# Output projection of a tile pair in seven block products instead of eight, with sums of rows and their low parts on VectorE

## The reference, cut to what matters

```
q, k, v = heads(x @ Wq + bq), heads(x @ Wk + bk), heads(x @ Wv + bv)     # 16 heads of 32
scores = where(mask == 0, -inf, einsum(q, k) / sqrt(32))
out = einsum(softmax(scores), v)                                        # back to 128 x 64 x 512
return layernorm(x + out @ Wo + bo)                                     # no gain, no shift, eps 1e-5
```

## Time and profile before

| | |
|---|---|
| median of 3 runs | 822.24 us (821.85 to 822.4) |
| profiled execution: its own time | 821.39 us |
| its span | 819.5 us |
| granted TensorE clock, mean | 0.999 |
| TensorE matmul busy | 812.0 us, 99% |
| VectorE, GpSimd, ScalarE busy | 544.9, 512.6, 238.2 us |

### The profile page before, as it was taken

How to read it: one execution, slowest core, us unless ns; L and a number is a source line. 1 busy time by engine, 2 the same in 40 slices (tenths; PEclk the granted TensorE clock), 3 DMA queues, 4 the chain that set the end, 5 groups by cost and what they waited for, 6 DMA issues and landing times.

```text
span 819.5 us, 25422 instructions
## 1 busy us (share of the span) xinstructions
PE 812.0 (99%) x11286; PEld 665.1 (81%) x11286; DVE 544.9 (66%) x691; ACT 238.2 (29%) x315; POOL 512.6 (63%) x407
## 2 busy tenths in 40 slices
PE   9999999999999999999999999999999999999997
PEld 7788888888888888888888888888888888888886
DVE  5667667766567666676665776656766567766795
ACT  6532233221332222332223322133322233223223
POOL 1386667656675565856658566576665767657682
PEclk9999999999999999999999999999999999999999
DMA  9224424253342433424334243352424434234342
GB/s 321 90 79 122 120 81 135 84 143 95 88 143 72 149 92 92 139 70 142 105 91 134 71 144 95 82 154 82 128 88 106 136 82 131 84 108 118 105 105 104
DMA packets 50173, 92.37 MB, mean 113 GB/s; under 512 B 11280, under 2 KB 13328, under 8 KB 47888
## 3 DMA queue, kind: packets, MB, share of 16 engines
q1 hardware_dynamic: 47568, 87.08, 36.2%
q10 hardware_dynamic: 2496, 3.67, 1.6%
HBM read 40.37 MB, written 16.78 MB: 70 GB/s over the span
## 4 chain that ended last, share of the span: by engine, by line
PE 98%; DVE 1%; POOL 0%; ACT 0%; issue 0%; POOLq 0%; DVEq 0%
PE ring L289 23%; PE ring L291 21%; PE ring L290 21%; PE ring L386 7%; PE ring L387 7%; PE ring L390 7%; PE psum_s L357 6%; PE ring L375 6%; PE ring L407 1%; PE ring L309 0%; POOL soft L912 0%; PE ring L313 0%; PE ring L317 0%; DVE soft L717 0%; DVE top L724 0%; ACT soft L568 0%
## 5 line engine op out<-in xcount | busy, mean ns | idle before, releaser
L912 POOL TENSOR_TENSOR soft<-soft,top 128x1024 f32<-128x1024 f32 x62 | 125.2, 2020 | 77.5 <-DVE top L724 77.5
L171 POOL TENSOR_TENSOR soft<-soft,inverse 128x1024 f32<-128x1024 f32 x62 | 118.9, 1918 | 24.9 <-DVE inverse L731 22.2
L563 ACT ACTIVATE kt<-ring,bk 128x512 f32<-128x512 f32 x64 | 43.6, 681 | 258.7 <-PE ring L291 258.6
L889 POOL TENSOR_TENSOR x_lo<-x_raw,x_hi 128x512 fp32r<-128x512 f32 x56 | 72.0, 1286 | 61.1 <-ACT x_hi L548 61.1
L289 PE MATMUL ring<-wv_hi,x_hi 128*128 128x512 f32 x256 | 103.5, 404 | 0.0
L289 PE MATMUL ring<-x_hi,wk_hi 128*128 128x512 f32 x256 | 103.1, 403 | 0.0
L728 DVE TENSOR_REDUCE total<-soft 128x16 f32<-128x1024 f32 x62 | 75.6, 1219 | 41.0 <-ACT soft L568 41.0
L291 PE MATMUL ring<-wv_hi,x_lo 128*128 128x512 f32 x256 | 100.1, 391 | 0.0
L291 PE MATMUL ring<-x_hi,wk_lo 128*128 128x512 f32 x256 | 99.9, 390 | 0.0
L290 PE MATMUL ring<-x_lo,wk_hi 128*128 128x512 f32 x256 | 99.7, 390 | 0.0
L290 PE MATMUL ring<-wv_lo,x_hi 128*128 128x512 f32 x256 | 99.6, 389 | 0.0
(11 more groups left out here) (81 smaller groups left out, 1362.3 us busy)
## 6 DMA issues: line engine op xcount, KB each, us to landing
pt<-soft SPq DMA_DIRECT2D x464, 64.0 KB, 2.0
x_raw<-in_xt SPq DMA_DIRECT2D x15, 1024.0 KB, 6.8
row<-in_x SPq DMA_DIRECT2D x60, 256.0 KB, 2.7
out_rows<-row SPq DMA_DIRECT2D x60, 256.0 KB, 2.6
adj<-in_adj SPq DMA_DIRECT2D x16, 128.0 KB, 2.9
pt<-soft ACTq DMA_DIRECT2D x32, 64.0 KB, 2.2
kt<-in_wk SPq DMA_DIRECT2D x4, 256.0 KB, 5.1
row<-in_wv SPq DMA_DIRECT2D x1, 1024.0 KB, 8.4
```

What stands on the lines that cost most here:

```text
L171: ops.tensor_tensor(soft_of(c), soft_of(c), on_keys(inverse[:, c % 2, :]), ALU.mult).then_inc(normed, 1)
L889: nc.gpsimd.tensor_tensor(x_lo[:, buf, :, rows], x_raw[:, :, rows], x_hi[:, buf, :, rows].bitcast(F32), ALU.subtract).then_inc(x_lo_done, 1)
L912: nc.gpsimd.tensor_tensor(soft_of(c), soft_of(c), on_keys(top[:, c % 2, :]), ALU.subtract).then_inc(centred, 1)
```

## The change

The output projection of the two tiles of a pair is a product of a 256 x 512 matrix of rows by the 512 x 512 matrix Wo. Both are cut into 2 x 2 blocks (tile by half of the features; half of the features by half of the columns), and for the first 27 pairs the eight block products become seven: three of them take sums of blocks of rows (`s`) by sums of blocks of weights (`t`), one takes a sum of rows by a plain block, one a plain block by a sum of weights, two plain blocks. A block product is 2 chunks by 3 parts: six matmuls of 256 columns. The sums of weights are made once, at the start, on GpSimd and ScalarE. For each pair ScalarE copies the mixed rows to SBUF, VectorE makes four sums of rows, ScalarE their high parts, VectorE their low parts. The products of a pair are done in three places: four between q of b+4 and v of b, one after the next scores, two after k of a+4. Two of the first four go to bank 0 of the scores. VectorE adds the results to the row buffers in six instructions, by quarters and halves of a row, in place of two.

Beside this: the bias is kept once and not four times over, so that a tile's mask is two instructions of 512 elements, not one of 1024; ScalarE normalises the rows of all these pairs; GpSimd's additions of bo are put after `centre(a)` and after `normalise(a)` and concern the pair before; rows are stored and loaded after both `place` of an iteration, and the first four are loaded at the start; `pt` has two buffers, not four, and the second one holds the raw mixed rows in between; q of b+4 is projected after v of a, and ScalarE reads it after the sums' high parts.

```diff
+            def product(out, left_hi, left_lo, right_hi, right_lo, adds=False):
+                for kc in range(2):
+                    nc.tensor.matmul(out, left_hi[:, kc, :], right_hi[:, kc, :], start=kc == 0 and not adds, ...)
+                    nc.tensor.matmul(out, left_hi[:, kc, :], right_lo[:, kc, :], start=False, ...)
+                for kc in range(2):
+                    last = nc.tensor.matmul(out, left_lo[:, kc, :], right_hi[:, kc, :], start=False, ...)
+            def first_products(m):
+                pe.wait_ge(masked, 4 * (m + 2))
...
+                product(first_bank()[:, 0:HALF], *rows_block(0, 1), *weights_block(1, 0))
+                product(first_bank()[:, HALF:D], *rows_block(1, 1), *weights_sum(4)).then_inc(y_part, 1)
+                product(ring[:, 2, 0:HALF], *rows_block(0, 0), *weights_block(0, 0)).then_inc(y_part, 1)
+                pe.wait_ge(s_hi_done, m + 1)
+                pe.wait_ge(s_lo_done, m + 1)
+                product(ring[:, 3, 0:HALF], *rows_sum(1), *weights_sum(1)).then_inc(y_part, 1)
+            def middle_product(m):
+                pe.wait_ge(row_part, PARTS * m + P1)
+                product(ring[:, 2, 0:HALF], *rows_sum(2), *weights_sum(2), adds=True).then_inc(y_part, 1)
+            def last_products(m):
+                pe.wait_ge(row_part, PARTS * m + P6)
+                product(ring[:, 2, 0:HALF], *rows_sum(3), *weights_sum(3), adds=True).then_inc(y_part, 1)
+                product(ring[:, 3, 0:HALF], *rows_sum(4), *weights_block(1, 1), adds=True).then_inc(y_part, 1)
@@ TensorE, iteration p
                 score(a)
                 score(b)
+                if p >= 2:
+                    middle_product(p - 2)
                 pe.wait_ge(v_done, a - 1)
                 project_k(a + 4)
+                if p >= 2:
+                    last_products(p - 2)
                 pe.wait_ge(v_done, a)
                 project_q(a + 4)
                 pe.wait_ge(k_done, a + 5)
                 project_k(b + 4)
-                pe.wait_ge(q_done, a + 5)
-                project_q(b + 4)
-                wait_for(pe, row_added, a - 2)
+                wait_for(pe, row_part, PARTS * (p - 1))
                 mix(a - 2)
                 mix(b - 2)
                 pe.wait_ge(k_done, b + 5)
                 project_v(a)
+                pe.wait_ge(q_done, a + 5)
+                project_q(b + 4)
+                first_products(p - 1)
                 pe.wait_ge(q_done, b + 5)
                 project_v(b)
-                pe.wait_ge(ot_lo_done, p)
-                project_out(a - 2)
-                project_out(b - 2)
@@ ScalarE, iteration p
                 read_k(a + GT), exp(a), read_q(a + GT), exp(b), read_k(b + GT)
-                read_q(b + GT)
-                read_ot(p - 1)
+                read_pair(p - 1)       # mixed rows to SBUF, then their high part
+                split_sums(p - 1)      # s_hi, 1024 elements
+                read_q(b + GT)
                 for c in (a, b):
+                    norm_by_act(c - 4)
                     split_x(c + 2 * GT)
@@ VectorE
+            def split_blocks(m):
+                nc.vector.tensor_tensor(ot_lo[:, 0], ot_raw()[:, 0], ot_hi[:, 0].bitcast(F32), ...)
+                nc.vector.tensor_tensor(ot_lo[:, 1, 2:4, :], raw_block(1, 1), ot_hi[:, 1, 2:4, :].bitcast(F32), ...)
+            def add_rows(m):
+                nc.vector.tensor_tensor(s_raw(m, 2), raw_block(0, 0), raw_block(1, 0), ALU.subtract)
+                nc.vector.tensor_tensor(s_raw(m, 0), raw_block(1, 0), raw_block(1, 1), ALU.add)
+                split_blocks(m)
+                nc.vector.tensor_tensor(s_raw(m, 1), s_raw(m, 0), raw_block(0, 0), ALU.subtract)
+                nc.vector.tensor_tensor(s_raw(m, 3), raw_block(0, 1), s_raw(m, 1), ALU.subtract)
+            def split_sums(m):         # s_lo, 1024 elements, two operands in SBUF
@@ VectorE, iteration p (from p = 2 on)
-                add_row(a - 3), mask(a), mask(b), norm_row(a - 3), sum_up(a), sum_up(b), turn(a), turn(b),
-                split_ot(p - 1), read_v(a), read_v(b), add_row(a - 2), norm_row(a - 2)
+                mask(a), add_sixth(p - 2), mask(b), sum_up(a), add_last(p - 2), sum_up(b), turn(a),
+                row_sums(a - 4), add_rows(p - 1), read_v(a), split_sums(p - 1), turn(b), add_first(p - 1),
+                row_sums(b - 4), add_middle(p - 1), read_v(b)
@@ GpSimd, iteration p (from p = 2 on)
-                make_rstd(a - 3), centre(a), centre(b), normalise(a), normalise(b), add_bo(a),
-                make_bias (even p), split_x(a + 8), split_x(b + 8), add_bo(b), make_rstd(a - 2)
+                centre(a), add_bo(a - 2), centre(b), normalise(a), add_bo(b - 2), normalise(b),
+                make_shift(a - 4), make_shift(b - 4), make_bias (even p), split_x(a + 8), split_x(b + 8)
@@ GpSimd, start
+            add_weights()              # four sums of blocks of Wo, 128 x 512 each, two of them in a chain
+            split_weight_sums()        # their low parts, four of 128 x 512
@@ SyncE, iteration p
-                store(a - 3), place(a), load_row(b), place(b), store(a - 2), load_row(b + 1)
+                place(a), place(b), store(a - 4), store(b - 4), load_row(a), load_row(b)
@@ score(c)
+                    if 2 <= c // 2 <= FULL:
+                        pe.wait_ge(row_part, PARTS * (c // 2 - 2) + P24)
```

More of the change, by code:

```diff
@@ L83, in attention_kernel @@
         shift = sb("shift", [P, 8, 1])
[L84 to L86 removed]
+        small = sb("small", [P, 14])
+        last_stats = small[:, 0:12].rearrange("p (n s) -> p n s", n=2)
+        eps, minus_half = small[:, 12:13], small[:, 13:14]
         psum_s = ctx.enter_context(nc.psum_tensor("psum_s", [P, HC, 2, 2, KC, SQ], F32))
@@ L178, in by_chunk, with ot_raw, raw_block, s_raws @@
             return ot[:, tiles, :, :].rearrange("p t c (g q) -> p (t c) g q", g=2)
+        def ot_raw():
+            return pt[:, 1].rearrange("p q h k -> p (q h k)").rearrange("p (t c n) -> p t c n", t=2, c=KC)
+        def raw_block(i, j):
+            return ot_raw()[:, i, 2 * j:2 * j + 2, :]
+        def s_raws(m):
+            return v[:, 2 * m % 4:2 * m % 4 + 2, :].rearrange("p t (n c q) -> p (t n) c q", n=2, c=2)
+        def s_raw(m, n):
+            return s_raws(m)[:, n]
+        def w_raw_block(i, j):
+            return w_raw[3][:, 2 * i:2 * i + 2, j * HALF:(j + 1) * HALF]
+        def t_raw(n):
+            return pt[:, n // 2, n % 2, :, :].rearrange("p h k -> p (h k)").rearrange("p (c n) -> p c n", c=2)
+        def quarter(m, i, j):
+            return row[:, (2 * m + i) % 4, j * HALF:(j + 1) * HALF]
+        def first_bank():
+            return psum_s[:, 0].rearrange("p t b c k -> p (t b c k)")
         def ot_count(c):
@@ L248, in _ @@
             sp.wait_ge(w_lo_done, 3 * KC)
-            load_row(0)
+            for c in range(4):
+                load_row(c)
             for p in range(FULL):
@@ L392, in project_out @@
                 last.then_inc(y_proj, 1)
+            def product(out, left_hi, left_lo, right_hi, right_lo, adds=False):
+                for kc in range(2):
+                    nc.tensor.matmul(out, left_hi[:, kc, :], right_hi[:, kc, :], start=kc == 0 and not adds, stop=False,
+                                     skip_group_check=adds)
+                    nc.tensor.matmul(out, left_hi[:, kc, :], right_lo[:, kc, :], start=False, stop=False,
+                                     skip_group_check=adds)
+                for kc in range(2):
+                    last = nc.tensor.matmul(out, left_lo[:, kc, :], right_hi[:, kc, :], start=False, stop=kc == 1,
+                                            skip_group_check=adds)
+                return last
@@ L596, in place, with split_weight_sums @@
                         act.dma_start(to, of).then_inc(pt_in[c % 4], DMA)
+            def split_weight_sums(n):
+                act.wait_ge(t_raw_done, 4)
+                nc.scalar.copy(t_hi[:, n], t_raw(n)).then_inc(t_hi_done, 1)
             def split_w(n, kc):
@@ L638, in _ @@
             split_w(3, 3)
+            for n in range(4):
+                split_weight_sums(n)
             for p in range(FULL):
@@ new lines, in split_sums, with add_part, add_first @@
+            def split_sums(m):
+                dve.wait_ge(s_hi_done, m + 1)
+                nc.vector.tensor_tensor(s_lo[:, :, :, :], s_raws(m), s_hi[:, :, :, :].bitcast(F32),
+                                        ALU.subtract).then_inc(s_lo_done, 1)
+            def add_part(m, part, to, of):
+                dve.wait_ge(y_part, PARTS * m + part)
+                nc.vector.tensor_tensor(to, of, to, ALU.add).then_inc(row_part, 1)
+            def add_first(m):
+                to = row[:, 2 * m % 4:2 * m % 4 + 2, 0:HALF]
+                dve.wait_ge(row_biased, 2 * m + 2)
+                add_part(m, P24, to, first_bank().rearrange("p (t n) -> p t n", t=2))
+                dve.wait_ge(row_part, PARTS * m + P24)
```

(16 more changed lines are left out.)

229 lines of the change are left out of this document (162 added, 67 removed).

## The result

The changed kernel takes 833.12 us, median of 4 runs (831.45 to 833.85), beside 822.05 for the kernel before, measured again beside it (median of 4 as well): ratio 1.0132, interval 1.0115 to 1.015. Forecast were 814.4 us, in a range of 811.0 to 821.0. The profiled execution took 833.85 us, its span 832.0 at a granted clock of 0.998. 813.6 were laid out for it, so 20.25 us are to be found.

What follows compares the result with a forecast made beforehand. TensorE, busy 99% of the span, was taken as the bound. 821.39 - 10.8 (products) + 2.6 (x_lo stalls) + 0.4 (start) = 813.6 us profiled; the median, 0.85 above, was forecast at 814.4, range 811.0 to 821.0.

Steps and rivals of the forecast that it cites:

- Seven products: TensorE, per pair: 42 matmuls of 256 columns at 0.120 replace 24 of 512; gain 0.40 us, 10.8 over 27 pairs.
- The 7.6 us of restarts: TensorE, product groups not following the scores: small-to-large changes could cost 27 x 0.28 = 7.6 us at most; taken as 0.
- Weight loads: Rival, TensorE: weight loads of 188 ns bind short matmuls, a pair takes 7.90, +66 us, 889 us; chance 0.02 (or the like).
- SyncE: Main loop queue: second place ends at t = 2, stores and loads bring a row by 6.5, when GpSimd wants it.
- the rival of the shared operands: VectorE instructions with two SBUF operands slow beside GpSimd by 890/692: stall 1.35 us per group, 829.4 us; chance 0.11.
- The wait for x_lo: Even iterations, first k of a group: TensorE idles 0.2 us for GpSimd's x_lo, 13 times, 2.6 us.
- VectorE: Main loop: net +3.7 us per pair, 27 times 100 us, about 645 us busy, 80% of the span; fits as a sum.
- Row sums at 425 ns: Sign of being right: VectorE's new row sums take 425 ns; 500 ns or more beside a busy GpSimd would show it wrong.
- Start and end: Start: GpSimd's sums and low parts make the first centre late, +0.4 us (0 to 1.5); end: extra statistics and norms, 0.
- The rivals: Whole kernel: no stall 811.8 us (0.20), shared operand path 829.4 (0.11), half of it 818 to 822 (0.12), weight loads 889 (0.02).
- stalls of 0.55 to 0.8: Rival "half of it": such stalls per group, from the operand meeting or handovers between products, give 818 to 822 us; chance 0.12.
- four low parts of 1.29: Start, GpSimd: four low parts of 512 elements, about 1.29 us each, follow ScalarE's copies and run 30.4 to 35.4.

Runs made afterwards that it cites:

- run 1: Changed kernel, with SyncE issuing the store of a-4 before place(b) and the load of row a right behind place(b): 816.44 us, ratio 0.9929.
- run 2: Changed kernel, with split_x ahead of make_shift(b-4) on GpSimd and x_hi of b+8 ahead of ScalarE's norm of b-4: 833.86 us, ratio 1.0135.
- run 8: Changed kernel with SyncE's store and row load earlier, split_x ahead of make_shift(b-4), and add_bo(b-2) behind normalise(b): 820.07 us, ratio 0.9972.
- run 3: Version with both edits: changed kernel with SyncE's store and row load earlier and split_x ahead of make_shift(b-4): 816.08 us, ratio 0.9922; measured again 817.72 us.
- Run 4: Changed kernel, with GpSimd's add_bo(a-2) moved from between centre(a) and centre(b) to behind normalise(a): 822.17 us, ratio 0.9995.

## Why the prediction was wrong, step by step

**Seven products: right.** 256-column starts 0.120 apart, and undisturbed iterations of 24.81 to 24.93 where 24.77 was laid out and 25.17 stood before. Of the 0.1 over, 0.08 stands at the scores (1.60 for 1.52) and 0.02 in the sum of the other parts (24.79); 2.7 us in all. The 7.6 us of restarts that bounded this from above did not come. Weight loads did not bind: the rule of the Trainium skill weighed in the prediction (TensorE: Matmul & The Clock Gate, Part 3, The mechanism), that a load overlaps matmuls in flight only where the row group differs, is contradicted by the changed kernel as by the one before. The prediction left out that the same section also lets a load be pulled ahead when it goes to the background weight buffer; the 0.120 us agree with that sentence, though no run here shows which buffer a load takes.

**SyncE: this step failed.** The prediction had the second place end at t = 2, "and the stores and row loads behind it bring a row by 6.5, just when GpSimd wants it", under the heading of what is cheap or hidden. In iteration 16, one of the better ones (scores at 454.88), the rows of SyncE and GpSimd are:

```profile
444.07 12.46 SPq L264 DMA_DIRECT2D pt<-soft  x16
456.57 1.96 SPq L280 DMA_DIRECT2D out_rows<-row  x2
459.92 0.96 SPq L273 DMA_DIRECT2D row<-in_x  x2
```
```profile
459.36 1.92 POOL L1135 TENSOR_TENSOR soft<-soft,top 128x1024 f32<-128x1024 f32 x1 [1.31 <-DVE top L868]
462.73 1.30 POOL L1131 TENSOR_TENSOR row<-row,bo 128x512 f32<-128x512 f32 x1 [1.44 <-DMA row<-in_x]
```

The places end at 456.53, t = 1.65: that was right. GpSimd is through with `centre(a)` at t = 6.40: right too. But the row comes at t = 7.85. From the end of the places it takes 6.2 us and not 4.5: 2.0 for issuing two stores, 1.4 until the store has landed and releases the load, 2.8 for the load. That is 1.35 us of error in a term with no slack beside it. The 4.5 rested on no row, and the page of the kernel before would have given more. Its part 6 (KB each, median us from issue to landing) has

```profile
row<-in_x SPq DMA_DIRECT2D x60, 256.0 KB, 2.7
out_rows<-row SPq DMA_DIRECT2D x60, 256.0 KB, 2.6
```

which is 5.3 for a store and the load behind it. Worse than the size was the reading. "Just when it is wanted" is a tie, and a tie in a chain that returns to its own start is no hidden cost: `centre(b)` was queued behind the addition, and through it the exponential, the transposes and the next places. In the bad iterations the places themselves then come late: in iteration 9 they end at t = 4.67. The prediction priced every chain against TensorE's iteration and never asked whether the last link leads to the first. It did see the link: the rival of the shared operands mentions "A delay of `centre(b)` by a late row load" and gives it 0.15 us, for the meeting of the instructions alone.

**The wait for x_lo: there, mis-sized, and not a cause.** 13 stalls of 0.2 were foreseen, 10 came of 0.4 to 1.0, and 8.8 us stand at that place. Of the 0.18 us a stall, the 0.05 for the semaphore came from no row: in all ten, 0.145 us pass from the end of x_lo to the matmul, and the restart costs 0.08 (the next matmul starts 0.305 later, not 0.227). The chain laid out for it is right in its links; it starts at the end of mixing with ScalarE's copy, and this copy stood behind the late exponential (265.48 above). With the row on time, 0.4 us remain of it (run 1), fewer than the 2.6 of the forecast; without the chain but with the row late, the total does not move (run 2).

**VectorE.** Forecast 645 us busy, measured 621.5, since it added lengths and the records of instructions in a row overlap, often by about 0.08 us: added up, VectorE's lengths grow by 105 us (559.7 to 664.3), close to the forecast's 100, the busy time only by 77. "Row sums at 425 ns" holds for the second (412), not for the first (751), which meets GpSimd's late `normalise`.

**Start and end.** +0.4 us was forecast, by a late `centre`; iteration 0 is 0.36 longer (16.77 for 16.41). The first scores are 0.76 later before that, which the forecast did not have (0.2 to 1.1 later in the runs above). Iteration 2 waited 1.43 us for row parts, which the forecast did not have.

**The rivals.** The shared path gave 829.4 us and had the right sign by the wrong mechanism: run 8 prices it at 2.4 to 4.0 us where the loop is open, and what it adds inside the loop is not shown. The step that mattered was in no rival, and all of them argued about the forward path of an iteration. With the load order mended the change takes 816.1 to 817.7 us. 814.4 is then short by 1.7 to 3.3: the 0.1 us per iteration named above and the stall that did not come nearly cancel (+2.7 and -2.6), and what is left lies in the profile of run 3 mostly at the ends, where the forecast had nothing but its 0.4: first scores 1.08 later than in the kernel before, iteration 0 longer by 0.15, iteration 2 at 25.44, and some 0.8 in iteration 1 and behind the main loop. Two sums of the prediction are slightly off and change nothing: stalls of 0.55 to 0.8 give 819.0 to 822.2, not 818 to 822, and four low parts of 1.29 take 5.2 us, not the 5.0 from 30.4 to 35.4.

What stays open: why issuing 8 DMAs of a tile takes anything from 4.9 to 7.3 us, how much of the 16.7 us went through the lengthened row sum inside the loop, and what delays the first two iterations by some 2 us in the version with both edits.

## What to carry to other kernels

Follow each chain of an iteration on until it either ends or comes back to where it began; a chain that comes back is a second bound beside the busiest engine, and every wait in it (a store that must land before its buffer is loaded, a queue that issues in order) counts at full length. When several engines wait a little and the waits wander from one kernel variant to the next, look for the loop and not for the largest wait. A load that depends on a store belongs behind other work of the queue, with the store ahead of that work: here that order alone turned 1.3% slower into 0.7% faster.

## What the runs showed of the hardware

**Two operands in SBUF: beside GpSimd's `normalise`, VectorE's sum waits for its end.** A row sum on VectorE takes 0.41 to 0.43 us by itself. In the version with both edits, first pair:

```profile
62.09 1.62 DVE L909 TENSOR_TENSOR v<-pt 128x256 f32<-128x256 f32 x1
63.64 0.41 DVE L910 TENSOR_TENSOR v<-pt 128x256 f32<-128x256 f32 x1
```
```profile
61.50 1.93 POOL L195 TENSOR_TENSOR soft<-soft,inverse 128x1024 f32<-128x1024 f32 x1
```

The sum is issued at 62.09 and ends at 63.71, about 0.3 us after GpSimd's instruction ends at 63.43: it did not run slower, it waited 1.2 us and then ran. Run 4 shows it best: when the first sum is issued, GpSimd's instruction still has anything from 0.24 to 1.71 us to go, and in all 27 pairs the sum ends 0.28 to 0.29 us after it. The ratio of 890 to 692 ns from which the prediction priced the meeting is thus the wrong form; the price is what is left of the other's instruction. The 890 was a mean of one instruction of 1519 ns and three of 680. The other way round, GpSimd's one-element shift, 0.27 us, takes 0.80 to 0.82 beside VectorE's sums and ends 0.05 us after one of them. The Trainium skill, SBUF — State Buffer, Who interferes with whom, says just this of a VectorE instruction with two inputs in SBUF and a GpSimd one that reads SBUF: the shared ports go to one of them for a whole instruction, and the second to come is blocked until the first is done. The trace agrees for these instructions, but not for all: in the kernel before, GpSimd's TENSOR_SCALAR that makes the bias runs from 18.47 to 22.12, and four wv_lo on VectorE, issued from 18.54 on, end at 20.06, 20.66, 21.26 and 21.86, all before it; only the first was held up. By the page's rule the rival of the prediction would have been priced at the overlap of the two schedules and not at a ratio, which is right for `normalise`.

**Issuing DMAs has a size of its own.** One tile's 8 transfers of 64 KB occupy SyncE's queue for 4.9 to 7.3 us in the main loop (9.5 once, in iteration 1); two stores took 1.08 us in iteration 8 and 1.96 in iteration 16.
